# One vision-transformer block on one core: V alone goes through HBM, and a tile's residual rows are fetched back behind the next tile's store

## What is computed

```python
h = einsum('bnp,dp->bnd', patches, W) + b          # 768 -> 256
h = concatenate([cls_tok, h], axis=1)              # 50 tokens per image
x = layernorm(h); qkv = x @ Wqkv.T + bqkv          # 256 -> 768
qkv = qkv.reshape(B, 16, S, 48)                    # a plain reshape, no transpose
q, k, v = split(qkv, 3, axis=-1)                   # 16 numbers each
attn = softmax(q @ k.T / 4); vals = (attn @ v).reshape(B, S, 256)
h = h + vals @ Wo.T + bo
h = h + ffn(layernorm(h))                          # relu, fp8-like rounding of hidden and w2
```

## Time and profile before

| | before |
|---|---|
| median of 3 runs | 113.52 us (113.03 to 113.63) |
| the profiled execution's own time | 114.19 us |
| its span, first to last instruction | 112.4 us |
| mean granted TensorE clock, as a share of full speed | 0.969 |
| TensorE busy | 102.8 us, 91% of the span |
| DVE, ACT, POOL busy | 69.4, 52.2, 56.7 us |
| bytes moved by DMA | 15.14 MB |

### The profile page before, as it was taken

One profiled execution on the slowest core, in us unless ns is written; L12 is line 12 of the kernel. 1 busy time (PEld: TensorE's weight loads), 2 busy tenths in 40 slices (PEclk: granted clock), 3 DMA queues, 4 the chain that ended last, 5 costly groups with the idle time before them and its releaser, 6 DMA issues.

```text
span 112.4 us, 3831 instructions
## 1 busy us (share of the span) xinstructions
PE 102.8 (91%) x1547; PEld 89.3 (79%) x1547; DVE 69.4 (62%) x132; ACT 52.2 (46%) x113; POOL 56.7 (50%) x94
## 2 busy tenths in 40 slices
PE   6999999999982999899999979999998999999970
PEld 6997665789752899889798869898897879899860
DVE  5001975899866156969898995997793724410050
ACT  2622244098550471356628226458469265335500
POOL 8399325999897200677953073079241443330040
PEclk9999999999999656999999999999999999999999
DMA  3999995428716826626336516532540010040013
GB/s 67 352 397 414 397 385 183 140 61 156 238 46 121 253 75 106 222 46 132 124 109 123 202 30 126 217 46 48 192 43 30 6 39 0 15 113 5 0 39 89
DMA packets 21433, 15.14 MB, mean 135 GB/s; under 512 B 14312, under 2 KB 17704, under 8 KB 21416
## 3 DMA queue, kind: packets, MB, share of 16 engines
q1 hardware_dynamic: 20696, 14.24, 42.9%
q10 hardware_dynamic: 720, 0.67, 2.0%
HBM read 9.89 MB, written 5.02 MB: 133 GB/s over the span
## 4 chain that ended last, share of the span: by engine, by line
PE 69%; DMA 7%; DVE 5%; POOL 4%; SPq 4%; issue 4%; ACT 3%; DVEq 0%; ACTq 0%; POOLq 0%
PE psum L440 10%; PE psum L441 9%; PE psum L442 9%; PE psum L659 6%; PE psum L558 6%; DMA v_rows<-qkv_sb 5%; PE psum L601 5%; PE psum L475 5%; PE psum L681 5%; PE psum L581 3%; PE psum L447 3%; SPq L419 3%; POOL x_lo L1199 2%; PE psum L537 2%; DMA v_sb<-v_rows 2%
## 5 line engine op out<-in xcount | busy, mean ns | idle before, releaser
L1078 ACT ACTIVATE x_sb<-psum,cols 128x200 fp8e4<-128x200 f32 (+2 forms) x24 | 11.6, 484 | 17.2 <-PE psum L659 9.8
L1257 POOL TENSOR_TENSOR vals<-att,rsum 128x256 f32<-128x256 f32 x8 | 5.0, 622 | 24.9 <-DVE rsum L869 24.9
L822 DVE SCALAR_TENSOR_TENSOR qkv_sb<-psum,rstd,bqkv_sb 128x768 f32<-128x768 f32 x8 | 8.1, 1018 | 6.7 <-PE psum L442 3.4
L1059 ACT ACTIVATE probsT<-psum 128x400 f32<-128x400 f32 x16 | 7.3, 506 | 6.9 <-PE psum L581 6.9
L440 PE MATMUL psum<-w_hi 128*128 128x250 f32 (+1 forms) x32 | 10.3, 321 | 0.0
L905 DVE TENSOR_TENSOR x_sb<-psum,b_q 125x256 f16<-125x256 f32 (+1 forms) x7 | 3.0, 422 | 11.7 <-PE psum L681 11.6
L601 PE MATMUL psum<-probsT,v_sb 64*32 64x50 f32 (+1 forms) x512 | 7.3, 205 | 3.0 <-DMA v_sb<-v_rows 2.8
L847 DVE TENSOR_REDUCE rmax<-psum 128x16 f32<-128x800 f32 x8 | 7.8, 981 | 3.4 <-PE psum L558 3.4
L601 PEld LDWEIGHTS psum<-probsT,v_sb 64*32 64x32 f32 (+1 forms) x512 | 6.2, 107 | 4.4 <-DMA v_sb<-v_rows 3.0
L442 PE MATMUL psum<-w_hi,w_lo 128*128 128x250 f32 (+1 forms) x32 | 9.6, 301 | 0.0
L441 PE MATMUL psum<-w_lo,w_hi 128*128 128x250 f32 (+1 forms) x32 | 9.6, 300 | 0.0
(11 more groups left out here) (96 smaller groups left out, 271.7 us busy)
## 6 DMA issues: line engine op xcount, KB each, us to landing
v_rows<-qkv_sb SPq DMA_DIRECT2D x8, 384.0 KB, 4.0
x_sb<-in_xt SPq DMA_DIRECT2D x6, 294.0 KB, 8.2
h_rows<-h_bo SPq DMA_DIRECT2D x8, 128.0 KB, 3.4
w_sb<-in_w1t SPq DMA_DIRECT2D x2, 512.0 KB, 5.7
w_sb<-in_w2t SPq DMA_DIRECT2D x4, 256.0 KB, 3.2
v_sb<-v_rows SPq DMA_DIRECT2D x32, 25.0 KB
w_sb<-in_wt SPq DMA_DIRECT2D x3, 256.0 KB, 3.7
wqkv_sb<-in_wqkvt SPq DMA_DIRECT2D x2, 384.0 KB, 5.6
```

The costliest lines, as they stand in the source:

```text
L822: dve.scalar_tensor_tensor(qkv_sb[:, t % 2].rearrange("p (n c) -> p n c", n=2), p_wide[:, :, 0:QKV // 2], rstd[:, 0, t % 2:t % 2 + 1], bqk ...
L1078: act.activation(hq[:, m, first:end], p_wide[:, ff1_bank[n], 0:end - first], ACT.Relu, bias=b1_col[:, m:m + 1], saturate=False).then_inc(h ...
```

## The change

`Wqkv`'s rows and `bqkv` are reordered on the host: first the 16 pairs of Q and K (512 columns), then the 16 V's (256 columns). In `qkv_sb` V is thus a dense block of its own. SP stores that block alone; `v_rows` shrinks from 768 to 256 columns, and `v_keys` reads pieces of 16 floats that lie side by side. `turn_q` and `turn_k` read dense runs (for `turn_k` shifted by 16). And SP's order in the loop changes: the fetch of tile t - 1's tokens comes right behind the store of V(t), and the wait for `h0bo_done(t)` with the store of `h_rows[t]` comes at the loop's end, behind V's loads and the weight load; the last tile's tokens are fetched after the loop.

```diff
+QK = HEADS * 2 * HD
...
         def v_keys(s, j):
-            rows = v_rows[s, 32 * j:32 * j + QTOK].rearrange("n w -> (n w)").rearrange("(u q e) -> q u e", q=TOKENS, e=CHUNK)
-            return rows[:, :, 2 * HD:]
+            rows = v_rows[s, 32 * j:32 * j + QTOK].rearrange("n w -> (n w)")
+            return rows.rearrange("(u q e) -> q u e", q=TOKENS, e=HD)
...
                 if t >= 2:
                     sp.wait_ge(v_in[s], 16 * QUADS * (t // 2))
-                sp.dma_start(v_rows[s], qkv_sb[:, s]).then_inc(v_stored, 16)
-                sp.wait_ge(h0bo_done, t + 1)
-                sp.dma_start(h_rows[t], h0_bo[:, t]).then_inc(h0_stored, 16)
+                sp.dma_start(v_rows[s], qkv_sb[:, s, QK:]).then_inc(v_stored, 16)
+                if t >= 1:
+                    move_tokens(t - 1)
                 sp.wait_ge(v_stored, 16 * (t + 1))
...
                     sp.dma_start(w2_sb[:, kc, :], w2t[:, kc, :]).then_inc(w2_in[n // 2], 16)
-                move_tokens(t)
+                sp.wait_ge(h0bo_done, t + 1)
+                sp.dma_start(h_rows[t], h0_bo[:, t]).then_inc(h0_stored, 16)
+            move_tokens(TILES - 1)
...
-                by_chunk = qkv_sb[:, t % 2].rearrange("p (c e) -> p c e", e=CHUNK)
-                dve.transpose(qT[:, t % 2].rearrange("p (n c) -> p c n", c=HEADS),
-                              by_chunk[:, :, 0:32]).then_inc(qT_done, 1)
+                by_chunk = qkv_sb[:, t % 2, 0:QK].rearrange("p (c e) -> p c e", e=32)
+                dve.transpose(qT[:, t % 2].rearrange("p (n c) -> p c n", c=HEADS), by_chunk).then_inc(qT_done, 1)
...
-                by_chunk = qkv_sb[:, t % 2].rearrange("p (c e) -> p c e", e=CHUNK)
-                dve.transpose(kT[:, t % 2, LEAD:].rearrange("p (n c) -> p c n", c=HEADS),
-                              by_chunk[:, :, HD:HD + 32]).then_inc(kT_done, 1)
+                by_chunk = qkv_sb[:, t % 2, HD:HD + QK].rearrange("p (c e) -> p c e", e=32)
+                dve.transpose(kT[:, t % 2, LEAD:].rearrange("p (n c) -> p c n", c=HEADS), by_chunk).then_inc(kT_done, 1)
...
+    by_chunk = np.arange(QKV).reshape(HEADS, CHUNK)
+    order = np.concatenate([by_chunk[:, 0:2 * HD].reshape(-1), by_chunk[:, 2 * HD:].reshape(-1)])
+    wqkv, bqkv = np.asarray(L0_attn_Wqkv)[order], np.asarray(L0_attn_bqkv)[order]
```

More of the change, by code:

```diff
@@ L1330 @@
         "wt": blocks(np.asarray(L0_tok_W).T),
-        "wqkvt": blocks(np.asarray(L0_attn_Wqkv).T),
-        "wqkv_rows": np.asarray(L0_attn_Wqkv).reshape(P, QKV // P, D),
+        "wqkvt": blocks(wqkv.T),
+        "wqkv_rows": wqkv.reshape(P, QKV // P, D),
         "wot": blocks(np.asarray(L0_attn_Wo).T),
@@ L1337 @@
             [column(L0_tok_b), column(cls_tok), column(L0_ffn_b1)], axis=1)),
-        "bqkv_rows": rows(L0_attn_bqkv, P),
+        "bqkv_rows": rows(bqkv, P),
         "bo_rows": rows(L0_attn_bo, P),
@@ L1346 @@
     h_rows = nc.dram_tensor("h_rows", (TILES, P, D), F32, kind="Internal").ap()
-    v_rows = nc.dram_tensor("v_rows", (2, P, QKV), F32, kind="Internal").ap()
+    v_rows = nc.dram_tensor("v_rows", (2, P, QKV - QK), F32, kind="Internal").ap()
     out = nc.dram_tensor("out_0", (IMAGES * TOKENS, D), F32, kind="ExternalOutput").ap()
```

## The result

The changed kernel takes 108.68 us (median of 4, 108.17 to 109.24), the kernel before 113.28 us beside it (112.82 to 113.63). The ratio is 0.9597, with a 95% interval of 0.9535 to 0.9659: 4.6 us, 4% faster. In two later comparisons it was 0.9576 (0.9531 to 0.9621) and 0.9565 (0.9499 to 0.9631).

A forecast was written before the change was run, and what follows sets the result against it. TensorE bounds the kernel, with one hole before attend(1) and a slow-clock stretch behind it. 2.77 us idle less 0.4, plus 3.05 clock, less 0.3, taken as 5.1: 109.1 profiled, 108.4 us median; range 107.5 to 111.6.

The forecast's parts named there:

- SP's order: SP queue, tiles 0 and 1: V(1)'s store issued at about 23.4 instead of 26.54, its loads at 27.4.
- The bound with the old landing of 6.14 us: V(1) landing as slowly as before: attend(1) could start at 32.9, or 34.4 with V(0) slow; hole at worst 1.2 us.
- What is late next: TensorE before scores(2), waiting for DVE to turn K(2) until 34.75: up to 0.4 us of idle time left.
- The clock: TensorE at full clock in scores(2), qkv(3) and project(0), once the hole closes: 3.0 to 3.1 us saved.
- The clock rival: Hole closes, but thin work around it still lowers TensorE's clock, or it falls elsewhere: 3.05 us given back, 111.4; 14%.
- The schedule: New times after the hole: DVE's addition of attention at 39.2 instead of 44.24, turn_vals(1) at about 41.45 instead of 46.51.
- The stand for DVE's chain: TensorE standing a little for DVE's chain, which leads to turn_vals(1): 0.3 us subtracted from the gain.
- POOL's chain: V(0)'s loads meeting ACT's wmean broadcast, delaying POOL's halves for qkv(3): 1.2 us to spare; counted within the forecast.
- The transposes: DVE's turning of Q and K from a dense run: nothing taken; at best 0.36 us each, 5.5 in all.
- Only V is stored: SP's store cut from 384 KB to 128 KB: no gain of its own, since V(1) isn't late with either landing.
- V(1) comes too late: Rival: with landings over 6.4 us attend(1) waits again, 1 to 1.5 us: 109.5 to 110; 8%.
- The slower rival: SP waits for h_rows(t - 1) ahead of V(t)'s loads in tiles 3 to 6: 114.8 at 2.7 us delay; 5%.

The follow-up runs named there:

- the pair with and without idle products: Changed kernel with V(1)'s loads held until tile 2's QKV is scaled: 114.32 us; the same with 30 idle products in the hole: 111.44 us.
- the kernel with the extra store: Changed kernel, but Q and K (256 KB per tile) also stored into a tensor nobody reads, V's loads waiting for both stores: 110.44 us, ratio 0.9659.
- the kernel whose two profiles show 1.3 and 1.1 us: Changed kernel with SP's old order, V alone stored: 111.53 us, ratio 0.968; run a second time: 110.78 us, ratio 0.9774.

## Why the prediction was right, point by point

The forecast was 108.4 us, the measurement 108.68, and it came about in the main by the forecast's own steps:

- **SP's order.** V(1)'s store at 23.4: it was 23.18. Its loads at 27.4: 27.49. I had taken the near end for V(0)'s landing, 2.5 us; its loads went out 3.8 us behind the store, at 19.72, which still left time before h0 + bo. The bound with the old landing of 6.14 us wasn't tested: even the full store landed within 4.6 us in the new order. (Its two figures, 32.9 and 34.4, should be 32.8 and 34.3.)
- **What is late next.** Up to 0.4 us in front of `scores(2)`: 0.48.
- **The clock.** 3.05 us; the pair with and without idle products says 3.0 by its traces, 2.5 to 2.9 by its times, and the kernel before with idle products 2.8 by its trace. The clock rival is refuted: without a hole the same thin work leaves the clock at 1.00, and with idle products in the hole too.
- **The schedule.** `turn_vals(1)` at 41.45: 41.57, 4.94 us earlier than before. DVE's addition of attention at 39.2: 39.32. The stand for DVE's chain is 0.50 us, and it was 0.28 before.
- **POOL's chain** was not pushed: its halves for `qkv(3)` began at 32.79, where they had begun at 33.03.
- **The transposes.** No gain: their row in the changed kernel is the one below.

```profile
L836 DVE STREAM_TRANSPOSE qT<-qkv_sb x8: 1029/1071/1082, 15.9 to 72.7; 128x512 f32<-128x512 f32 x8
```

The median was 1056 before. A dense source changes nothing. The Trainium skill (Vector Engine (DVE) Microarchitecture Reference, The reshape front-end and per-opcode configuration) gives a transpose one element per cycle per lane. No run here shows that pace; if something keeps the row above it, it is not the source's layout, and the strided destination was not tried.

**The term that was wrong** is in "Only V is stored": I gave the smaller store no gain, because V(1) would be in time either way. That holds for tile 1 in the new order, but it isn't the whole price of traffic: the ratios put the store's size at 0.4 and 0.8 us, and the kernel with the extra store at 1.1. Each of the three is hardly clear of its intervals, but all have the same sign. I had also not seen that in the old order the smaller store alone would shorten the hole by more than half.

**Where the number had luck.** The forecast gain was 5.1 us and the measured one 4.6. The forecast came out only 0.3 us too low because the starting point was lower as well: the kernel before had 113.28 us in the comparison, where I had started from 113.52. In the profiles the span shrank by 5.5 us, 4.9 of it up to `turn_vals(1)` and 0.5 as the shorter stand near 60 us, 0.26 instead of 0.72; but the profiled execution of the kernel before was 0.9 us above that median. Medians of the kernel before in the other comparisons were 113.6 to 113.8, and against these the changed kernel's gain is 5.2 to 5.3 us.

On the landings the Trainium skill (DMA: Bandwidth & Descriptors, Anatomy of one DMA) would have given 0.6 us, an estimate; its fit is for DMAs that GpSimd issues, while SP issues these. The median in the profile went from 4.0 to 3.3 us:

```profile
DMA to landing us min/median/max: 1.7/3.3/4.0
```

That is about as much, but the order changed as well, and the medians of the changed kernel's three profiles are 3.3, 2.6 and 3.4 us. With the order kept the median went from 4.0 to 3.7 us, and in the new order it is 3.5 and 3.7 with the full store. V(1)'s own landing, with the order kept, went from at most 6.1 to at most 4.7 us and saved more than the estimate; why is not shown.

**The rivals.** That V(1) comes too late didn't happen, but the margin is smaller than I thought: the four issues took 2.87 us, not 1.69. By my estimate V(1) was there about 0.9 us ahead of `attend(1)`, where I had reckoned with 2.5. The slower rival had the right mechanism (SP standing for h_rows with V behind it) and the right reason why it doesn't bite: the rows were stored an iteration before. Take that away, and the kernel is 6% slower than the kernel before.

## What to carry to other kernels

When a queue does several round trips through HBM per tile, write down for each wait what stands behind it in program order; a finished tile that waits for a queue which waits for someone else's result is the first thing to look for. Put a landing's consumer one iteration later rather than right behind it: the same order with the fetch in its own iteration cost 11 us more. And price a hole of TensorE at its own length, less the waits behind it that it swallows, plus the slow stretch that may follow: here a hole of 3 us cost 2.1 to 2.5 and 3.0 us.

## What I had not expected of the hardware

- The hole of 2.8 to 3.0 us in front of `attend(1)` took the clock down in every execution (mean 0.954 to 0.970). At the same place a hole of 1.7 us did it in three executions of four, and the kernel whose two profiles show 1.3 and 1.1 us had a mean clock of 0.967 to 0.981 in six of ten; the others kept it at 0.995 or more with the same program. Such a kernel's times scatter by 2 to 3 us.
- The length of the hole isn't all that counts. Elsewhere, stands of 1.6 us (right behind the idle products in the kernel before), and of 1.4 and 1.7 us (`attend` at 74.87 and 84.26 in the kernel that fetches its own rows) left the clock at 1.00. What tells these from the others was not tried.
- Idle products keep the clock at 1.00 through a wait of over 3 us: 2.5 to 2.9 us off for two lines, even with `attend(1)` 0.5 us later, counted from the piece ahead of it.
- From the first issue of V(1)'s loads to the start of `attend(1)` it took 3.3 us in the kernel before (32.68 to 35.96), and 3.3 to 3.4 in every other profile in which `attend(1)` waits for V without idle products, but 4.9 us in the kernel before with idle products (32.40 to 37.30). Other DMAs, issued behind the loads on the same queue, were in flight in both; what held V up was not tried.
- Four load issues on SP, 1.7 to 1.9 us in the kernel before, took between 1.7 and 3.2 us in the changed kernel. What lengthens them was not tried.
